# Expert tiles aligned to the end of each expert's rows in a transformer kernel's expert stage

## The reference

```python
scores = jax.nn.softmax((xf @ gate_w), axis=-1)              # 4096 tokens, 8 experts
_, sel = jax.lax.top_k(scores + expert_bias[None, :], 2)
order = jnp.argsort(sel.reshape(-1), stable=True)            # 8192 routed rows
routed_in = xf[order // 2] * top_scores_sorted[:, None]
h = silu(ragged_dot(routed_in, w1, counts)) * ragged_dot(routed_in, w3, counts)
routed_out = ragged_dot(h, w2, counts)
out = (silu(xf @ sw1) * (xf @ sw3) @ sw2).at[order // 2].add(routed_out)
```

## Time and profile before

| | us |
|---|---|
| median of 3 runs | 2492.61 (2486.66 to 2495.77) |
| time of the profiled execution | 2490.43 |
| its span on the core | 2488.8 |
| PE busy | 2031.3 (82%) |
| DVE busy | 1919.5 (77%) |
| ACT busy | 1520.0 (61%) |
| POOL busy | 1515.5 (61%) |

### The profile page before, as it was taken

One profiled execution on the slowest core, in us unless ns is written; L12 is line 12 of the kernel. 1 busy time (PEld: TensorE's weight loads), 2 busy tenths in 40 slices (PEclk: granted clock), 3 DMA queues, 4 the chain that ended last, 5 costly groups with the idle time before them and its releaser, 6 DMA issues. The chain is left out here.

```text
span 2488.8 us, 60316 instructions
## 1 busy us (share of the span) xinstructions
PE 2031.3 (82%) x19761; PEld 1513.7 (61%) x19761; DVE 1919.5 (77%) x4927; ACT 1520.0 (61%) x2859; POOL 1515.5 (61%) x2351
## 2 busy tenths in 40 slices
PE   8965788787788888888887699788499958869887
PEld 5634556565565566565565588666255536659887
DVE  4547999999999999999999454456433329969998
ACT  5657999999999999999997122255122213323222
POOL 2446888989899888898898223244111135525554
PEclk9986998999999999999998799888699979989999
DMA  5776776776767766767766367544222224521110
GB/s 165 243 217 167 192 181 170 193 185 173 192 178 188 187 175 175 189 177 187 193 178 159 93 194 231 165 134 144 85 85 83 85 82 140 153 90 46 51 52 30
DMA packets 295158, 373.66 MB, mean 150 GB/s; under 512 B 44628, under 2 KB 234647, under 8 KB 294903
## 3 DMA queue, kind: packets, MB, share of 16 engines
q1 hardware_dynamic: 284710, 342.05, 49.5%
q0 software_dynamic: 9872, 27.28, 3.5%
q10 hardware_dynamic: 320, 1.05, 0.2%
HBM read 151.03 MB, written 85.00 MB: 95 GB/s over the span
## 5 line engine op out<-in xcount | busy, mean ns | idle before, releaser
L760 PE MATMUL p_ps_sc<-p_CR,p_BR 64*128 64x128 f32 x4096 | 314.2, 294 | 141.5 <-DVE p_M L1061 91.7
L674 POOL TENSOR_TENSOR p_CR<-p_pc 128x256 f32<-128x256 f32 x512 | 373.9, 730 | 71.1 <-DVE p_pc L1044 58.3
L678 POOL TENSOR_TENSOR p_BR<-p_pb 128x256 f32<-128x256 f32 x512 | 373.9, 730 | 31.4 <-DVE p_pb L1053 13.4
L760 PEld LDWEIGHTS p_ps_sc<-p_CR,p_BR 64*128 64x128 f32 x4096 | 268.5, 197 | 200.2 <-issue 151.7
L906 ACT ACTIVATE p_D<-p_ps_x 128x512 f32<-128x512 f32 x512 | 289.2, 592 | 70.3 <-PE p_ps_x L726 68.7
L1061 DVE TENSOR_TENSOR p_M<-p_ps_sc,p_D 128x1024 f32<-128x1024 f32 x256 | 310.2, 1212 | 9.6 <-issue 5.6
L1044 DVE SCALAR_TENSOR_TENSOR p_pc<-p_ps_c,p_beta,p_cs 128x256 f32<-128x256 f32 x512 | 242.4, 473 | 34.4 <-issue 18.7
L775 PE MATMUL p_ps_y<-p_M,p_uexp 128*32 128x128 f32 x4096 | 254.6, 279 | 0.0
L1053 DVE SCALAR_TENSOR_TENSOR p_pb<-p_ps_b,p_beta,p_cs 128x256 f32<-128x256 f32 x512 | 242.1, 473 | 0.0
L1053 DVE SCALAR_TENSOR_TENSOR p_pb<-p_ps_b,p_beta,p_sn 128x256 f32<-128x256 f32 x512 | 242.1, 473 | 0.0
L1044 DVE SCALAR_TENSOR_TENSOR p_pc<-p_ps_c,p_beta,p_sn 128x256 f32<-128x256 f32 x512 | 242.0, 473 | 0.0
(11 more groups left out here) (284 smaller groups left out, 5170.7 us busy)
## 6 DMA issues: line engine op xcount, KB each, us to landing
p_cs<-p_tr_c SPq DMA_DIRECT2D x256, 256.0 KB, 4.1
p_sn<-p_tr_s SPq DMA_DIRECT2D x252, 256.0 KB, 4.5
p_phib<-scratch_phi SPq DMA_DIRECT2D x256, 128.0 KB, 3.1
p_x<-scratch_rt SPq DMA_DIRECT2D x72, 128.0 KB, 2.0
scratch_ro<-p_o POOLq DMA_DIRECT2D x72, 128.0 KB, 2.0
p_xT<-in_xT SPq DMA_DIRECT2D x64, 128.0 KB, 4.6
scratch_u<-p_u SPq DMA_DIRECT2D x16, 512.0 KB, 3.4
scratch_wu<-p_wu SPq DMA_DIRECT2D x16, 512.0 KB, 4.3
```

What stands on the lines that cost most here:

```text
L674: e.tensor_tensor(CR[:, p, g, :], pc[:, g % 2, 0, :], pc[:, g % 2, 1, :], ALU.add).then_inc(S["rotC"], 1)
L678: e.tensor_tensor(BR[:, p, g, :], pb[:, g % 2, 0, :], pb[:, g % 2, 1, :], ALU.add).then_inc(S["rotB"], 1)
L760: m = e.matmul(sc_ps[half][:, (g * 2 + b) * L:(g * 2 + b + 1) * L], BR[half * 64:half * 64 + 64, p, 2 * q + g, b * L:(b + 1) * L], CR[half ...
```

## The change

In the new layout an expert's rows begin at row e * STRIDE + 128 of `rt`, behind 128 rows that are written with zeros. The tiles of an expert end with its last row; the padding lies in front, so the first tile begins inside the zero rows. The zeros are one more 1 MB DMA on POOL's queue, issued right behind the one that was there. The expert stage's eight zero writes, the waits around them and its zero tile are gone. SP loads the first four tiles right after the table, and the slots, `base` and `shift` behind these. DVE's slot instructions are spread over the first four steps. The table's chain is reordered (24 instructions), `shift` comes last in it, and SP writes the table before it waits for `shift`.

```diff
-TABLE = 2 * NTILE + NE
+TABLE = 2 * NTILE
@@ route_and_share, SP
-            e.wait_ge(S["tab_ok"], 5)
+            e.wait_ge(S["tab_ok"], 2)
             e.dma_start(W["tab"], tab[0:1, :]).then_inc(S["tab_out"], 16)
+            e.wait_ge(S["tab_ok"], 4)
             e.dma_start(W["shift"], shift[0:1, :]).then_inc(S["tab_out"], 16)
@@ route_and_share, POOL
             e.dma_start(W["rt"][NE * STRIDE:NE * STRIDE + NE * P, :].rearrange("(n p) d -> p n d", p=P),
                         repeat(zero[:, :], NE)).then_inc(S["zero_out"], 16)
+            e.dma_start(W["rt"][0:NE * STRIDE, :].rearrange("(n s) d -> s n d", s=STRIDE)[0:P, :, :],
+                        repeat(zero[:, :], NE)).then_inc(S["zero_out"], 16)
...
-            e.wait_ge(S["zero_out"], 16)
+            e.wait_ge(S["zero_out"], 32)
@@ route_and_share, DVE (parts of the chain)
+            e.memset(over[:, E:E + 1], -float(P)).then_inc(n, 1)
...
+            e.scalar_tensor_tensor(out=over[:, 0:E], in0=m0[:, :], scalar=-float(P), in1=cnt[:, :], op0=ALU.mult, op1=ALU.add).then_inc(n, 1)
...
-            e.tensor_tensor(tail[:, :], cnt[:, :], base[:, :], ALU.add).then_inc(n, 1)
...
+            e.tensor_copy(tab[:, NTILE:2 * NTILE], ej[:, :]).then_inc(made, 1)
+            e.wait_ge(n, NC + 17)
+            e.tensor_copy(tab[:, 0:NTILE], rj[:, :]).then_inc(made, 1)
+            e.tensor_tensor(first[:, :], up_to[:, :], m0[:, :], ALU.subtract).then_inc(n, 1)
...
+            e.tensor_tensor(m2[:, :], m1[:, :], over[:, 0:E], ALU.subtract).then_inc(n, 1)
+            e.wait_ge(n, NC + 20)
+            e.tensor_copy(shift[:, 0:1], m2[:, 0:1]).then_inc(made, 1)
+            e.tensor_tensor(shift[:, 1:E], m2[:, 1:E], m2[:, 0:E - 1], ALU.subtract).then_inc(made, 1)
@@ run_experts, SP
             e.dma_start(tab[:, :], W["tab"]).then_inc(S["tab_in"], 16)
-            e.dma_start(slots[:, :].rearrange("p (c n) -> p c n", c=NC), W["slot"].rearrange("c p n -> p c n")).then_inc(S["slots_in"], 16)
-            e.dma_start(base[:, :], on_all_partitions(I["c_base"])).then_inc(S["slots_in"], 16)
-            e.dma_start(shift[:, :], on_all_partitions(W["shift"][0, :])).then_inc(S["slots_in"], 16)
             e.wait_ge(S["tab_in"], 16)
-            e.wait_ge(S["prep"], 1)
-            for i in range(NE):
-                r = e.value_load(tab[0:1, 2 * NTILE + i:2 * NTILE + i + 1], min_val=0, max_val=NE * STRIDE)
-                e.dma_start(W["rt"][bass.ds(r, P), :], zero[:, :]).then_inc(S["tails_out"], 16)
-            e.wait_ge(S["tails_out"], 16 * NE)
...
             for i in range(NX):
                 load(i, i)
+            e.dma_start(slots[:, :].rearrange("p (c n) -> p c n", c=NC), W["slot"].rearrange("c p n -> p c n")).then_inc(S["slots_in"], 16)
+            e.dma_start(base[:, :], on_all_partitions(I["c_base"])).then_inc(S["slots_in"], 16)
+            e.dma_start(shift[:, :], on_all_partitions(W["shift"][0, :])).then_inc(S["slots_in"], 16)
@@ run_experts, POOL
-            e.memset(zero[:, :], 0.0).then_inc(S["prep"], 1)
@@ run_experts, DVE
             turned_x(0, 0)
+            step(0, 0)
             e.wait_ge(S["slots_in"], 48)
             e.tensor_tensor(over[:, :, :], spread(slots[:, :], NE), repeat(base[:, :], every), ALU.is_ge).then_inc(S["row_ok"], 1)
+            step(1, 1)
             e.tensor_tensor(over[:, :, :], over[:, :, :], repeat(shift[:, :], every), ALU.mult).then_inc(S["row_ok"], 1)
+            step(2, 0)
             e.tensor_reduce(move[:, :], over[:, :, :], mybir.AxisListType.X, ALU.add)
+            step(3, 1)
             e.tensor_tensor(slots[:, :], slots[:, :], move[:, :], ALU.add)
             e.tensor_copy(row[:, :, :].rearrange("p c n -> p (c n)"), slots[:, :])
-            step(0, 0)
-            step(1, 1)
-            with e.Fori(1, NTILE // 2 - 1) as j:
+            with e.Fori(2, NTILE // 2 - 1) as j:
@@ laid_out
-    A["c_base"] = np.arange(NE, dtype=f) * STRIDE
+    A["c_base"] = np.arange(NE, dtype=f) * STRIDE + P
```

More of the change, by code:

```diff
@@ L1555, in route_and_share @@
         xr = sb("xr", [P, 2, BATCH, DM])
-        cnt, m0, m1 = sb("cnt", [P, E]), sb("m0", [P, E]), sb("m1", [P, E])
+        cnt, m0, m1, m2 = (sb(n, [P, E]) for n in "cnt m0 m1 m2".split())
         up_to = sb("up_to", [P, E])
@@ L1560, in route_and_share @@
         ej, gone, ij, rj = (sb(n, [P, NTILE]) for n in "ej gone ij rj".split())
-        tail = sb("tail", [P, E])
+        over, drop = sb("over", [P, E + 1]), sb("drop", [P, 2, E])
         first, shift = sb("first", [P, E]), sb("shift", [P, E])
@@ L1804, in _ @@
             e.tensor_copy(cnt[:, :], pos_ps[:, 0:E]).then_inc(n, 1)
-            e.wait_ge(n, NC + 1)
+            e.memset(over[:, E:E + 1], -float(P)).then_inc(n, 1)
+            e.wait_ge(n, NC + 2)
             e.tensor_scalar(m0[:, :], cnt[:, :], 1.0 / P, 127.0 / 256.0, ALU.mult, ALU.add).then_inc(n, 1)
-            e.wait_ge(n, NC + 2)
+            e.wait_ge(n, NC + 3)
             e.tensor_scalar(m1[:, :], m0[:, :], MAGIC, None, ALU.add).then_inc(n, 1)
-            e.wait_ge(n, NC + 3)
+            e.wait_ge(n, NC + 4)
@@ L1816, in _ @@
[L1816 to L1821, removed]
+            e.tensor_tensor(drop[:, 0, :], over[:, 1:E + 1], over[:, 0:E], ALU.subtract).then_inc(n, 1)
@@ L1822, in _ @@
+            e.wait_ge(n, NC + 9)
             e.tensor_tensor(past[:, :, :], spread(tiles[:, :], E), repeat(up_to[:, :], NTILE), ALU.is_ge).then_inc(n, 1)
-            e.wait_ge(n, NC + 7)
-            e.tensor_tensor(before[:, :, :], past[:, :, :], repeat(m0[:, :], NTILE), ALU.mult).then_inc(n, 1)
+            e.scalar_tensor_tensor(out=drop[:, 1, :], in0=m0[:, :], scalar=-float(P), in1=drop[:, 0, :], op0=ALU.mult, op1=ALU.add).then_inc(n, 1)
+            e.wait_ge(n, NC + 11)
+            e.tensor_tensor(before[:, :, :], past[:, :, :], repeat(drop[:, 1, :], NTILE), ALU.mult).then_inc(n, 1)
@@ L1825, in _ @@
             e.tensor_reduce(ej[:, :], past[:, :, :], mybir.AxisListType.X, ALU.add).then_inc(n, 1)
-            e.wait_ge(n, NC + 9)
+            e.tensor_scalar(rj[:, :], tiles[:, :], float(P), float(P), ALU.mult, ALU.add).then_inc(n, 1)
+            e.wait_ge(n, NC + 14)
             e.tensor_reduce(gone[:, :], before[:, :, :], mybir.AxisListType.X, ALU.add).then_inc(n, 1)
-            e.tensor_scalar(rj[:, :], tiles[:, :], float(P), None, ALU.mult).then_inc(n, 1)
-            e.wait_ge(n, NC + 11)
@@ L1830, in _ @@
-            e.scalar_tensor_tensor(out=rj[:, :], in0=gone[:, :], scalar=-float(P), in1=rj[:, :], op0=ALU.mult, op1=ALU.add).then_inc(n, 1)
-            e.wait_ge(n, NC + 12)
-            e.tensor_tensor(tail[:, :], cnt[:, :], base[:, :], ALU.add).then_inc(n, 1)
-            e.wait_ge(n, NC + 13)
             e.scalar_tensor_tensor(out=ij[:, :], in0=ej[:, :], scalar=float(STRIDE), in1=rj[:, :], op0=ALU.mult, op1=ALU.add).then_inc(n, 1)
-            e.wait_ge(n, NC + 14)
-            e.tensor_copy(tab[:, 0:NTILE], ij[:, :]).then_inc(n, 1)
@@ L1837, in _ @@
-            e.tensor_copy(tab[:, NTILE:2 * NTILE], ej[:, :]).then_inc(n, 1)
-            e.tensor_copy(tab[:, 2 * NTILE:TABLE], tail[:, :]).then_inc(n, 1)
+            e.wait_ge(n, NC + 16)
+            e.scalar_tensor_tensor(out=rj[:, :], in0=gone[:, :], scalar=over[:, 0:1], in1=ij[:, :], op0=ALU.add, op1=ALU.add).then_inc(n, 1)
+            e.tensor_copy(tab[:, NTILE:2 * NTILE], ej[:, :]).then_inc(made, 1)
             e.wait_ge(n, NC + 17)
-            e.memset(gone[:, 0:1], 0.0).then_inc(made, 1)
@@ L1841, in _ @@
-            e.wait_ge(made, 5)
+            e.tensor_copy(tab[:, 0:NTILE], rj[:, :]).then_inc(made, 1)
+            e.tensor_tensor(first[:, :], up_to[:, :], m0[:, :], ALU.subtract).then_inc(n, 1)
+            e.wait_ge(n, NC + 18)
+            e.scalar_tensor_tensor(out=m1[:, :], in0=first[:, :], scalar=float(P), in1=base[:, :], op0=ALU.mult, op1=ALU.subtract).then_inc(n, 1)
+            e.wait_ge(n, NC + 19)
+            e.tensor_tensor(m2[:, :], m1[:, :], over[:, 0:E], ALU.subtract).then_inc(n, 1)
@@ L1855, in run_experts @@
         tab = sb("tab", [1, TABLE], mybir.dt.int32)
-        zero = sb("zero", [P, DM])
         x = sb("x", [P, NX, DM])
```

10 lines of the change are left out of this document (5 added, 5 removed).

## The result

Twelve runs of each kernel: 2477.65 us median (2472.78 to 2487.44) against 2489.34 (2485.58 to 2495.77) for the kernel before. The ratio is 0.9957, with a 95% interval of 0.9943 to 0.9971: 0.43% faster, 10.7 us (the two medians differ by 11.7). The interval leaves out 1, so the gain is real, and it is within the 0.5% that the prediction counted as no change. The forecast was 10.9 us less, and 2481.7. That figure is 4.0 above what was measured; 3.3 of them lie in the kernel before, whose median of three runs was 2492.61.

The account below looks back on a forecast made before the run. PE bounds the expert stage, but its start hangs on barrier, table, eight zero writes, their landing and first tile. The sum, -10.9 us and zeros, against the 2492.61 median gave 2481.7; range 2475.5 to 2487.0.

Parts of the forecast that it names:

- The zero writes: Start of the expert stage: without the eight writes ahead of the first tile's load, PE starts 10.9 us earlier (10.1 to 11.2).
- The three loads behind: Loads of slots, base and shift issued on SP behind four tile loads: cost zero, 1.2 us left; bound 1.4 us lost.
- The slot instructions: DVE's slot instructions spread over steps 0 to 3: each fits in 2.0 us of idle time a tile, cost zero.
- The table's chain: End of the routing stage: 24 instructions for 22, 0.6 us later at most, covered by POOL's drain with 3.3 us.
- PE's tiles: Expert stage, a sign to check in the changed kernel's profile: PE does its 72 tiles in 225 us.
- The second zero write: Head of the routing stage, on POOL's queue: cost taken as zero, 0.8 us kept as the nearer bound.
- (1): Rival: more comes out, from a shorter half-clock stretch of PE and an earlier table: 12.8 us saved, 2479.8; chance 0.12.
- (2): Rival: second zero write still in flight when chunk 2's loads go out: 7.4 us saved, 2485.2; chance 0.16.
- (3): Rival: something no row shows holds PE, or the drain grows by several us: half the gain, 2487.1; chance 0.07.
- (4): Rival: late chunk 2 leads PE into 15 long routing steps, costing 24 us: slower, 2505.7; chance 0.04.
- the sign that the prediction gave: Forecast is wrong if the routing stage, first load to barrier, changes its 164 us by more than 2.

Follow-up runs that it names:

- the four strided writes: Changed kernel plus three more 1 MB zero writes of the same strided shape in the routing stage; that stage took 170.4 us, 7.2 more.
- the first tiles ahead: Table kept in SBUF, plus first four tiles loaded beside POOL's drain and dequantizations behind steps 4 to 6; 2472.33 us, ratio 0.9927 to before.
- the table kept: Changed kernel with table, shift and base kept in SBUF across both stages; barrier to PE's first transpose 3.3 us in place of 4.6.

## Why the prediction was right

**The zero writes.** Right, 11.1 against 10.9, and not by luck: the writes put back account for 8.8, the three issues ahead of them for 1.1, and the rest is the forming of eight addresses. The unknown was the table's landing, taken as 1.5 us of a range from 1.2 to 2.2. With the first load 2.37 behind the table's issue and 1.10 for reading it, it is 1.3; kept in SBUF, the table saves that. Putting the writes back and doubling them showed that their price is SP's time. What the 1.10 consists of was not seen: 0.33 is the DMA's instruction, 0.27 the reading of the row, 0.16 the forming of the address from it.

**The three loads behind.** Right: `shift` was issued 7.8 us behind the table where 8.6 were forecast, mostly since the sum gives the last of the four loads 1.10 us where it takes its own 0.33 (the four took 3.67), and the compare began 0.1 us after DVE was free for it (rows below). The step that was mis-sized lies behind the margin: "each us by which these DMAs are later costs PE one". When DVE does have to wait there, PE's clock falls again, and 3.7 us of waiting cost 5.8, as the slot instructions in one piece showed.

**The slot instructions.** Right: the first of them sits in DVE's idle time, and so do the others (behind each DVE waits 1.4 us or more for ACT). DVE's timeline of the changed kernel, from tile 1's xT copy on; behind the compare it still waits 1.5 us for ACT (1.2 were forecast):

```profile
1789.56 0.42 DVE L1989 COPY p_xT<-p_ps_xt 128x256 f32<-128x256 f32 x1
1790.09 0.69 DVE L2012 TENSOR_TENSOR p_over<-p_slots,p_base 128x512 f32<-128x512 f32 x1
1792.31 0.39 DVE L1994 TENSOR_TENSOR p_h<-p_sa,p_ps_up 128x224 f32<-128x224 f32 x1 [1.52 <-ACT p_sa L1970]
```

**The table's chain.** Right that the drain hides it. Its 24 instructions took 6.3 us (1766.91 to 1773.17), no longer than 22 did; SP's end came 1.3 us behind POOL's drain start, well inside 5.5.

**PE's tiles.** The sign "its 72 tiles in 225 us" was misread from the earlier trace rows, a stretch that holds 847 of the stage's 864 matmuls: the 72 tiles took 230.4 before and 229.8 after. The forecast doesn't rest on it.

**The second zero write.** The cost was right, the step to it wrong: "the second has the DMA engines for itself". It was issued 1.2 us behind the first, and the two shared the engines with chunk 0's and 1's loads:

```profile
1622.00:1624.00 2.00, 2.00 (x6) 1.46 (x5) 1.23 (x10) 1.54 (x5) 0.00 (x0) 0.50 1.04 414
1624.00:1626.00 2.00, 2.00 (x6) 1.42 (x6) 1.73 (x13) 0.84 (x2) 0.00 (x0) 0.50 1.03 387
1626.00:1628.00 2.00, 2.00 (x14) 1.78 (x13) 0.43 (x1) 0.00 (x0) 0.00 (x0) 0.97 0.23 88
```

All 3 MB are through by about 1626.5, 5 us ahead of chunk 2's loads (1631.44). The Trainium skill ("DMA: Bandwidth & Descriptors", section "Latency and other measured facts") has row pitches of 4 MiB at half the rate and the same pitch with 4 KiB of padding at the full one. These rows have 387 GB/s, and the stretch with the four strided writes 338, so nothing was halved. That agrees with the page's exception for padded pitches, but it is no test of the rule. The page's pitch lies between neighbouring partitions; here neighbouring partitions are 1 KB apart, and the 4.1 MiB lie between the eight regions that each partition writes. The prediction did not see this difference.

POOL's drain is 0.08 us longer with the added write, the 0.1 that the prediction named as possible (last section).

**The rivals.** (1) has a small true part: the clock rose 5.7 us behind PE's start in place of 6.4, and PE's tiles took 0.6 less. That it is the change's doing is not shown: between profiles of kernels with the same matmuls the rise lies 4.3 (the first tiles ahead) to 7.2 us (the table kept) behind the start, and the tiles take 229.6 and 230.5 in these two. (2) can be made to happen, with three more megabytes. (3) did not happen, as PE's start moved by the chain's 11.1. (4) did not happen: the steps still alternate between 7.8 and 10.7 us, and the stage took 163.3. But the sign that the prediction gave, no more than 2 us off 164, was too fine: to the barrier the stage took 161.1 to 165.6 in the other kernels whose head was not loaded further (166.3 where POOL ends 1.4 us later), with no edit that would explain this spread. That it came out 1.1 off is in part luck.

## What to carry to other kernels

Where every engine stands behind a serial chain on one DMA queue, count what the queue's engine does for each: here eight writes cost 8 x 1.1 us and one landing, and less than a third of the 1.1 is the DMA's own instruction, the rest reading a row and forming an address. The work was free where that queue and the DMA engines had nothing to do. Where a load is moved behind others, the instruction that needs it must be able to wait. And what an idle gap costs is read between two events of the trace; the end-to-end times of this kernel spread by 15 us, more than the whole change.

## What the runs showed that I had not expected

POOL's drain at the end of the routing stage took 5.458 us in seven kernels, and 5.5 from the end of the last scatter's issue in the three where POOL didn't wait for the landing. It took 5.377 in the kernel before and with its writes doubled, and 5.703 with three more zero writes in the stage:

```profile
L1529 POOLq DRAIN  x1: 5703/5703/5703, 1764.2 to 1764.2; - x1
```

POOL issues 65 DMAs in this stage in the kernel before, 66 in the changed one and 69 with three more: 0.08 us more for each, and 0.083 us for each if the whole drain is divided by the count. The prediction had this as a guess that no row showed. The other stages of the kernel before fit: 5.93 us at the end of the expert stage with 72 DMAs of POOL, and in the stage behind it, with 64, a drain that ends 5.3 us behind POOL's last instruction, though its last DMA had been issued 25 us earlier; in a stage without any the drain took 0.66. So in these traces the drain goes with how many DMAs POOL issued in the block, not with how long ago they landed. Why it does is open, and a block with many fewer DMAs was not run.

A POOL that waits pays landing and drain in a row; letting SP wait was worth 1.6 us. Whether the drain at the end of the expert stage can be shortened the same way was not tried.
